# A Nyström attention and channel-mix block on one core: x's token statistics kept from part one, and both parts' loops written out

## The reference

```python
x = x + ln(attn(ln(x)))     # 16 heads of 16; 64 landmarks per head
x = x + ln(ffn(ln(x)))      # per sequence; token shift

def attn(h):
    q, k, v = heads(h @ Wq) / 4, heads(h @ Wk), heads(h @ Wv)
    q_l, k_l = mean of q and of k over 32 tokens each      # 64 landmarks
    s1, s2, s3 = softmax(q k_l'), softmax(q_l k_l'), softmax(q_l k')
    return merge(s1 @ (pinv(s2, 6 steps) @ (s3 @ v))) @ Wo + bo

def ffn(h):
    hp = h one token earlier (zero at the start)
    r = sigmoid((mu_r*h + (1-mu_r)*hp) @ W_r')
    k = (mu_k*h + (1-mu_k)*hp) @ W_k'
    return r * (relu(k)**2 @ W_v')
```

## Time and profile before

| what | us |
|---|---|
| three runs | 2111.35, 2111.69, 2116.46 |
| median | 2111.69 |
| the profiled execution | 2116.36 |
| its span | 2114.6 |
| PE busy | 1695.7 |
| PE weight loads | 1151.0 |
| DVE busy | 1481.7 |
| ACT busy | 1004.1 |
| POOL busy | 269.3 |

### The profile page before, as it was taken

One profiled execution on the slowest core, in us unless ns is written; L12 is line 12 of the kernel. 1 busy time (PEld: TensorE's weight loads), 2 busy tenths in 40 slices (PEclk: granted clock), 3 DMA queues, 4 the chain that ended last, 5 costly groups with the idle time before them and its releaser, 6 DMA issues.

```text
span 2114.6 us, 54815 instructions
## 1 busy us (share of the span) xinstructions
PE 1695.7 (80%) x21644; PEld 1151.0 (54%) x21644; DVE 1481.7 (70%) x3292; ACT 1004.1 (47%) x1679; POOL 269.3 (13%) x134
## 2 busy tenths in 40 slices
PE   2768857678468988898898879889898887988895
PEld 1557736678236546455555645555565555455553
DVE  8487776878773795689388658937873794688365
ACT  1157712686126535543654554455445535544652
POOL 4000000000300121021012101201120121021122
PEclk9879978799678999899899989989998999899997
DMA  5320010000221222121212211212212122121100
GB/s 156 95 77 3 3 62 11 2 3 4 76 48 41 56 51 73 44 51 50 66 51 50 62 55 42 58 52 64 53 37 81 26 51 74 44 60 40 48 31 30
DMA packets 125720, 104.91 MB, mean 50 GB/s; under 512 B 30368, under 2 KB 123424, under 8 KB 125472
## 3 DMA queue, kind: packets, MB, share of 16 engines
q1 hardware_dynamic: 124320, 99.29, 17.1%
q10 hardware_dynamic: 1152, 2.10, 0.3%
HBM read 56.23 MB, written 19.92 MB: 36 GB/s over the span
## 4 chain that ended last, share of the span: by engine, by line
PE 49%; DVE 27%; issue 13%; ACT 7%; POOL 2%; DMA 1%; DVEq 1%; ACTq 0%; POOLq 0%; SPq 0%
PE bank L1496 6%; PE bank L1288 4%; PE bank L1538 3%; PE bank L1516 3%; PE acc L1288 3%; ACT e L748 3%; PE bank L1475 3%; DVE m L1040 3%; DVE m L1032 2%; PE acc L1371 2%; PE bank L1299 2%; PE wide L1456 2%; DVE x2h L272 2%; PE wide L1393 2%; POOL xm L604 2%
## 5 line engine op out<-in xcount | busy, mean ns | idle before, releaser
L604 POOL TENSOR_TENSOR xm<-yy,xres 128x1024 f32<-128x1024 f32 x32 | 92.2, 2882 | 640.4 <-DVE yy L272 624.5
L1040 DVE TENSOR_REDUCE m<-wide 128x16 f32<-128x1024 f32 x128 | 149.9, 1212 | 21.2 <-PE wide L1335 21.2
L777 ACT ACTIVATE p<-wide 128x1024 f32<-128x1024 f32 x128 | 123.9, 1020 | 76.0 <-PE wide L1456 76.0
L748 ACT ACTIVATE e<-wide 128x1024 f32<-128x1024 f32 x128 | 130.3, 1024 | 62.4 <-PE wide L1393 57.7
L1032 DVE TENSOR_REDUCE m<-wide 128x2 f32<-128x1024 f32 x128 | 149.2, 1214 | 9.9 <-PE wide L1315 9.9
L1516 PE MATMUL bank<-wrT,xrT 128*128 128x256 f32 x512 | 124.8, 399 | 14.4 <-DVE ob L1126 9.7
L1538 PE MATMUL bank<-wvT,ka 128*128 128x256 f32 x512 | 126.8, 404 | 4.0 <-ACT ka L823 4.0
L1496 PE MATMUL bank<-wo,oT 128*128 128x256 f32 x512 | 120.5, 389 | 3.3 <-DVE oT L1075 2.6
L1062 DVE RECIPROCAL rr<-bank 128x4 f32<-128x4 f32 x16 | 2.8, 183 | 170.5 <-PE bank L1406 170.3
L620 POOL TENSOR_TENSOR ob<-ob,xm 128x1024 f32<-128x1024 f32 x32 | 76.5, 2391 | 353.0 <-DVE ob L272 353.0
L1516 PEld LDWEIGHTS bank<-wrT,xrT 128*128 128x128 f32 x512 | 98.8, 198 | 35.0 <-DVE ob L1126 8.4
(11 more groups left out here) (289 smaller groups left out, 4023.4 us busy)
## 6 DMA issues: line engine op xcount, KB each, us to landing
x1in<-in_L_attn_x SPq DMA_DIRECT2D x8, 2048.0 KB, 13.4
xin<-in_L_attn_x SPq DMA_DIRECT2D x32, 512.0 KB, 4.7
k_stack<-kh SPq DMA_DIRECT2D x256, 64.0 KB, 2.2
xres<-in_L_attn_x SPq DMA_DIRECT2D x32, 512.0 KB, 4.0
out<-ob SPq DMA_DIRECT2D x32, 512.0 KB, 3.0
k_stack<-kl SPq DMA_DIRECT2D x128, 64.0 KB, 2.0
q_stack<-landmarks SPq DMA_DIRECT2D x192, 4.0 KB, 1.6
inverse<-X ACTq DMA_DIRECT2D x8, 256.0 KB, 2.4
```

The lines of the kernel that those rows point to most:

```text
L604: g.tensor_tensor(xm[c % 3][:, :, :], yy[:, :, :], xres[:, :, :], ALU.add).then_inc(xm_made, 1)
L748: sc.activation(e3[t % 2][:, :], wide[t % 2][:, :], ACT.Exp).then_inc(wide_drained[t % 2], 1)
L777: sc.activation(p1[:, 2 * j:2 * j + 2, :], wide[w][:, :].rearrange("p (a n) -> p a n", a=2), ACT.Exp).then_inc(wide_drained[w], 1)
L1040: v.tensor_reduce(m1[:, tiles, 2 * w:2 * w + 2, :].rearrange("p t q x -> p q t x"), wide[w][:, :].rearrange("p (q t x m) -> p q t x m", q= ...
```

## The change

Part one's `mv1` and `rstd1` become one tile for each of the 8 sequences and stay on chip in part two. Part two's `norm_x` is gone: stage `X` leaves DVE and ACT, and DVE's `XA` reads `mv1[b]` and `rstd1[b]`. SP keeps its `X` stage, which only issues loads. Every `Fori` of part one and part two becomes a Python loop, so the instructions of all rounds are written out, and each wait's target is a constant. The order of the stages is that of before. The core of the diff:

```diff
+        mv1 = [sb(f"mv1{n}", [P, L // P, 2]) for n in range(B)]
+        rstd1 = [sb(f"rstd1{n}", [P, L // P]) for n in range(B)]
...
-        mv1 = [sb(f"mv1{s}", [P, NTL, 2], c=part1) for s in ROWS]
-        rstd1 = [sb(f"rstd1{s}", [P, NTL], c=part1) for s in ROWS]
...
-        norm_x = Norm("norm_x", 2)
+        x_applied = sem("x_applied")
...
-            with eng.Fori(0, B - 1) as b:
+            for b in range(B - 1):
...
-            with sp.Fori(0, B // GR) as i:
+            for i in range(B // GR):
...
-                    sp.wait_ge(norm_x.applied, b * NC + c - 1)
+                    sp.wait_ge(x_applied, b * NC + c - 1)
...
-            with act.Fori(0, B // GR) as i:
+            for i in range(B // GR):
...
-            def stage_X(at, b, c):
-                if not (isinstance(b, int) and c < 2):
-
-                    act.wait_ge(norm_x.applied, b * NC + c - 1)
-                norm_x.root(act, b * NC + c, c)
...
-            with dve.Fori(0, B // GR) as i:
+            for i in range(B // GR):
...
-            def stage_X(at, b, c):
+            def stage_XA(at, b, c):
+                if not (b == 0 and c < 2):
+
+                    dve.wait_ge(xhat_read, b * NC + c - 1)
                 dve.wait_ge(x_in[c % 2], 16 * (b * 2 + c // 2 + 1))
-                norm_x.stats(dve, xin[c % 2], b * NC + c, c)
-
-            def stage_XA(at, b, c):
-                if not (isinstance(b, int) and c < 2):
-
-                    dve.wait_ge(xhat_read, b * NC + c - 1)
-                norm_x.apply(dve, xhat[c % 2], xin[c % 2], b * NC + c, c)
+                for t in range(NT):
+                    ins = v.tensor_scalar(xhat[c % 2][:, t, :], xin[c % 2][:, t, :], mv1[b][:, c * NT + t, 0:1],
+                                          rstd1[b][:, c * NT + t:c * NT + t + 1], ALU.subtract, ALU.mult)
+                ins.then_inc(x_applied, 1)
...
-            with pe.Fori(0, B // GR) as i:
+            for i in range(B // GR):
...
-                pe.wait_ge(norm_x.applied, n + 1)
+                pe.wait_ge(x_applied, n + 1)
```

More of the change, by code:

```diff
@@ L249, in stats @@
                 dve.wait_ge(self.stats_made, g + 1)
-                if not (isinstance(g, int) and g < self.copies):
+                if g >= self.copies:
                     dve.wait_ge(self.applied, g + 1 - self.copies)
@@ L467, in stage_X @@
                 if c == 0:
-                    if not isinstance(b, int):
+                    if b > 0:
                         sp.wait_ge(m3_max, b)
@@ L477, in stage_X @@
                     load_bd(kA_bd, False, 1, b, kA_bd_in)
-                elif isinstance(b, int) and c >= 2:
+                elif b == 0 and c >= 2:
                     load_x(b, c)
             def stage_XA(at, b, c):
-                if not isinstance(b, int) and c < 2:
+                if b > 0 and c < 2:
                     load_x(b, c + 2)
@@ L493, in stage_B1 @@
                                      src[32 * q:32 * q + 32, :, :]).then_inc(k_stack_in, 16)
-                if c == 1 and isinstance(b, int):
+                if c == 1 and b == 0:
                     sp.wait_ge(stack_cleared, 1)
@@ L512, in stage_W @@
             def stage_W(at, b, c):
-                if not isinstance(b, int):
+                if b < B - 1:
                     load_x(b + 1, 0)
@@ L637, in _ @@
                 sc.activation(w16[:, w, 0, :, :], src[:, :, :], ACT.Copy, scale=WS).then_inc(w16_hi, 1)
-            with act.Fori(0, B // GR) as i:
+            for i in range(B // GR):
                 for s in ROWS:
                     act.wait_ge(p_dve, of(dve_steps, i, "mv", s))
-                    sc.activation(ln1[s][:, :], mv1[s][:, :, 1], ACT.Ln, bias=EPS).then_inc(p_act, 1)
+                    sc.activation(ln1[s][:, :], mv1[i * GR + s][:, :, 1], ACT.Ln, bias=EPS).then_inc(p_act, 1)
                     act.wait_ge(p_act, of(act_steps, i, "ln", s))
-                    sc.activation(rstd1[s][:, :], ln1[s][:, :], ACT.Exp, scale=-0.5).then_inc(p_act, 1)
+                    sc.activation(rstd1[i * GR + s][:, :], ln1[s][:, :], ACT.Exp, scale=-0.5).then_inc(p_act, 1)
                 for s in ROWS:
@@ L834, in stage_GA @@
                 norm_f.root(act, n, c)
-            part2_program(act, {"X": stage_X, "GB": stage_GB, "R": stage_R, "A": stage_A, "V": stage_V,
+            part2_program(act, {"GB": stage_GB, "R": stage_R, "A": stage_A, "V": stage_V,
                                 "D": stage_D, "F": stage_F, "W": stage_W, "E1": lambda at, b, c: scores(at, c, 0),
@@ L877, in _ @@
                                         pool_w[:, M - TM:M].unsqueeze(1).to_broadcast([P, NTL, TM]),
-                                        rstd1[s][:, :].unsqueeze(2).to_broadcast([P, NTL, TM]),
+                                        rstd1[i * GR + s][:, :].unsqueeze(2).to_broadcast([P, NTL, TM]),
                                         ALU.mult).then_inc(p_dve, 1)
@@ L887, in _ @@
                     for t in range(NTL):
-                        ins = v.bn_aggr(mv1[s][:, t, :], st1[s][:, t, :])
+                        ins = v.bn_aggr(mv1[i * GR + s][:, t, :], st1[s][:, t, :])
                     ins.then_inc(p_dve, 1)
@@ L1139, in _ @@
             v.memset(x2T[:, :, 0:1], 0.0).then_inc(carry, 1)
-            part2_program(dve, {"X": stage_X, "R": stage_R, "TA": stage_TA, "XA": stage_XA, "OA": stage_OA,
+            part2_program(dve, {"R": stage_R, "TA": stage_TA, "XA": stage_XA, "OA": stage_OA,
                                 "NA": stage_NA, "GA": stage_GA, "A": stage_A,
```

## The result

The changed kernel takes 2045.56 us (median of 4 runs, 2045.3 to 2050.22); the kernel before took 2111.52 in the same comparison. The ratio is 0.9677, with a 95% interval of 0.9654 to 0.97. It is faster, by 66 us where 87 were forecast; 2045.56 lies inside the range of 2001 to 2050, near its upper end, and outside the forecast's own 2008 to 2042. Measured again beside the experiments, the same changed kernel came out at 2051.29 and 2050.96 us, ratios 0.9708 and 0.9722, so a gain of 62 to 66 us by the medians is the fair reading. Both of these lie just above the range: that the first measurement fell inside it owes something to luck.

A forecast was written before the change was run, and what follows sets the result against it. PE was taken to be held up by issue waits around branches back and by waits for `x2h` before `T`. 51 + 1.8 + 29.4 + 0.3 + 4.5 = 87 us off the 2111.7 median gave 2024 us, range 2001 to 2050.

The forecast's parts named there:

- the forecast's own 2008 to 2042: Whole kernel: range of the main case alone, given chance 0.76, from bounds on statistics, clock and other register costs.
- Branch waits before `D`, 19.8 us: Part two, PE before the products of D: six issue waits at branches back, 19.8 us, would go without the branch.
- Issue waits in `F`, 8.7 us: Part two, PE within the products of F: eight issue waits, 8.7 us, would go with the branch.
- So those waits belong to the branch: End of a round: PE's waits in F and before D, 28.5 us in all, come from the branch back.
- straight code waits as well: Rival, chance 0.06: PE waits for slowly streaming code elsewhere too, leaving 28.5 + 21 us; about 2074 us.
- 28.5 us: Part two, PE: price of the issue waits before D and in F together, 19.8 + 8.7 us.
- Clock behind the branch, 21 us: From D 0 to the first O: slow clock after a branch costs 3.5 us a round, times 6, 21 us.
- Rounding 49.5 up to 51: Branch waits plus clock summed to 49.5 us, a second way gave 52.6; the prediction took 51.
- Statistics, 29.4 us: Part two, before T: removing DVE's statistics of x shortens PE's wait for x2h, 4.2 us a round, 29.4 in seven.
- Register instructions in `F`, 4.5 us: ACT's pairs of exponentials in F: constant targets save 0.08 us a pair, 8 pairs, seven rounds, 4.5 us.
- Part one, 1.8 us: Part one's branch, where DVE's statistics open the second round: a loss of 1.79 us goes, 1.8 us gained.
- Run against median, 4.7 us: Profiled execution of before was 4.7 us above the median, partly branch waits, so the sum was applied to the median.

The follow-up runs named there:

- pe_straight: Kernel before, with part two's loop written out on PE alone and kept on the other engines; 2083.3 us, ratio 0.9874.
- pe_loop: Kernel before, with part two's loop written out on ACT, DVE, POOL and SP while PE keeps its loop; 2114.3 us, ratio 1.001.
- half_pv: Changed kernel with half of F's products of e and vv left out in 14 of 16 tiles; 2033.5 us, ratio 0.9607.
- xin_early: Changed kernel with the next sequence's two xin chunks loaded at GA 0, mid-round, not at the end of F; 2033.6 us, ratio 0.9619.
- combined: Changed kernel with p_zero waited for once on DVE and ACT, and the next two xin chunks loaded at GA 0; 2030.0 us, ratio 0.9633.
- loops_no_stats: Kernel before, loops kept in both parts, part two's statistics of x left out; 2087.2 us, ratio 0.9871.

## Why the prediction was right, and where its sizes were off

The direction and the two mechanisms held; the sum was 21 us too large, and the range held it with 4 us to spare (the two later medians of 2051 would have missed it by 1). By its own steps:

- **Branch waits before `D`, 19.8 us:** right. All six are gone (at each of them a code packet had started only after PE had stopped), and `pe_straight` and `pe_loop` show that they are PE's alone.
- **Issue waits in `F`, 8.7 us:** the step that failed. "So those waits belong to the branch" rested on the end of the seventh round, where there was no branch and no wait: one case out of eight. The trace of before had a sign against it: two of the eight stand in the fourth round 9 and 14 us ahead of `D`, with more of `F` between them and the branch. In straight code the waits stay (10.7 us against 9.5, both lines), and most of their length needs both PE's pace in `F` and busy transfers beside it. Not all of it: ahead of the one 14 us before `D`, 0.5 us long, q1 had 6% of the engines. The rival "straight code waits as well" was right for this third of the 28.5 us, and I had tied it to the whole.
- **Clock behind the branch, 21 us:** mechanism right, size 16.9, and 10.5 and 15.6 in the two other profiles. With the waits in `F` still there, a round still enters `D` shortly after a gap. The three kernels with fewer of them give back 18.4 (`half_pv`), 19.4 (`xin_early`) and 22.2 (`combined`, 113.7 less 91.5). That is a correlation over whole kernels; single rounds don't follow it strictly (the 14.15 us at 1379.53 stand behind a wait of 1.69). Rounding 49.5 up to 51 had no ground either.
- **Statistics, 29.4 us:** right, 31.8 by `loops_no_stats`. The wait before `T` fell by 26.3 in the changed kernel, and the eight transposes behind it by 0.5 us a round, as costed, 3.7 in seven; some 2 us more aren't placed.
- **Register instructions in `F`, 4.5 us:** the gap of 0.08 us a pair is real and gone, but that it is worth time isn't shown. `pe_loop` has the short gaps and the rounds of before (1315.3).
- **Part one, 1.8 us:** the branch's 1.79 are gone, but I costed no second wait on the copies. It took some 5 us, so part one ended 2.9 us later in this profile, and some 2 on average over all.
- **Run against median, 4.7 us:** from profile to profile the gain is 71.1 us (2116.4 to 2045.3). That the excess of the profiled execution before was branch waits was a guess. The gain of the medians, 66.0, is smaller by 5.1, about that excess, so the forecast was too low by it.

Missing: `F` 8.7 and 1.2 more, clock 4.1 and the rounding 1.5, part one with `PRO` and `LAST` 2.7, the median 5.1, together 23; the statistics gave 2.4 more than costed, which leaves 21. The registers' 4.5 and some slower stretches (PE's issue waits before `M` grew from 5.1 to 6.7 us in seven) are inside what this sum can't separate.

## What to carry to other kernels

A hardware loop costs at its branch on the engine that is critical, here 3.1 to 4.9 us and a slow clock behind it (0.63 to 0.68 in these six stretches); write out that engine's loop first, since here the others could keep theirs. In straight code the next page of instructions is a transfer among the kernel's own, and it came up to 2.2 us late behind busy queues here, so keep large loads away from a stretch in which the critical engine issues many short instructions. And where constants replace registers, look at which instruction now carries the waits: one that is met once doesn't need repeating at every use.

## What was new of the hardware

- A DVE copy with two waits to meet, one of them met long before, started 0.103 us after the operation that it depends on, with a semaphore instruction of 21 ns between them; with one wait 0.034 us.
- A wait for code inside `F` stood behind the same product in two kernels and varied from 0.67 to 2.04 us with the transfers around it. Its end follows the start of a code packet by 2.2 to 2.6 us in 18 of 20 cases.
- At a branch back the code packet starts 0.5 to 0.7 us after PE has stopped. With `F`'s waits removed, the six waits at branches grew from 3.3 to 4.2 us each (19.8 to 25.0 in all), five of them with two code packets under way at once.
